# Two declarations moved in SBUF, so that matmul operands start at other offsets within a partition of SBUF

## What is computed

```python
xn = _layernorm(x)                       # x: (8, 512, 256)
# attention: q, k, v are two-layer nets with gelu
q = gelu(xn @ W1q + b1q) @ W2q + b2q     # k and v alike
scores = einsum('bid,bjd->bij', q, k) / sqrt(256 * 512) * tril(ones)
s = layernorm(einsum('bij,bjd->bid', scores, v)) * ln_w + ln_b
# feed-forward: weights quantised to -1, 0, 1 by their mean absolute value
h = relu(xn @ quant(W1).T + b1)          # 256 -> 1024
g = silu(h @ quant(W2).T + b2)           # 1024 -> 256
out = x + s * g
```

## The kernel before

| tensor | role in matmuls | before | after |
|---|---|---|---|
| `w_hi`, `w_lo`, `w1q` | stationary in L1, K, F1; moving in V (`w_*`) | 352 | 928 |
| `w2q` | moving in Y | 352 | 928 |
| `v_hi`, `v_lo` | moving in O | 352 | 416 |
| `x_all`, `xn`, `y`, `gw`, `v32` | none in the loop | 352 | 416 |
| `ident`, `ones`, `ones_r` | stationary in D (`ones_r`) | 128, 640, 128 | the same |
| `xT_*`, `g_*`, `r_*`, `z_*`, `e_*`, `s_*` | all the others | 928 | 928 |

## Time and profile before

### The profile page before, as it was taken

How to read it: one execution, slowest core, us unless ns; L and a number is a source line. 1 busy time by engine, 2 the same in 40 slices (tenths; PEclk the granted TensorE clock), 3 DMA queues, 4 the chain that set the end, 5 groups by cost and what they waited for, 6 DMA issues and landing times.

```text
span 312.9 us, 5715 instructions
## 1 busy us (share of the span) xinstructions
PE 306.3 (98%) x1874; PEld 272.8 (87%) x1874; DVE 248.0 (79%) x539; ACT 222.0 (71%) x420; POOL 133.3 (43%) x103
## 2 busy tenths in 40 slices
PE   8999999999999999999999999999999999999994
PEld 7688899888997899888997889978998889978894
DVE  3869988975899579895889759895798958596687
ACT  3486957959488667859489494886678595795862
POOL 2843673349060670509333390606705093313200
PEclk9799999999999999999999999999999999999999
DMA  7930035410004100050003200041000400020001
GB/s 249 372 121 0 2 111 157 136 70 0 2 2 138 63 0 0 34 168 0 0 0 125 76 0 0 0 138 63 0 0 35 167 0 0 0 69 2 0 2 67
DMA packets 15086, 18.54 MB, mean 59 GB/s; under 512 B 1761, under 2 KB 12513, under 8 KB 15074
## 3 DMA queue, kind: packets, MB, share of 16 engines
q1 hardware_dynamic: 14512, 17.98, 17.2%
q10 hardware_dynamic: 562, 0.41, 0.4%
HBM read 14.17 MB, written 4.22 MB: 59 GB/s over the span
## 4 chain that ended last, share of the span: by engine, by line
PE 74%; DVE 9%; issue 9%; POOL 4%; ACT 2%; DMA 1%; DVEq 0%; POOLq 0%
PE bank L810 73%; DVE gw L731 4%; POOL gw L359 2%; POOL o_rstd L353 2%; DVE g_lo L617 1%; DMA x_all<-in_x 1%; ACT o_square L484 1%; PE bank L792 1%; DVE e L642 1%; DVE x_all L733 1%; PE bank L839 1%; ACT o_var L487 1%; DVE gw L716 1%; DVE x_stats L547 0%; DVE gw L755 0%
## 5 line engine op out<-in xcount | busy, mean ns | idle before, releaser
L697 DVE TENSOR_TENSOR r_lo<-bank,r_hi 128x512 fp32r<-128x512 f32 x64 | 43.9, 691 | 34.4 <-ACT bank L464 34.4
L463 ACT ACTIVATE r_hi<-bank,col 128x512 fp32r<-128x512 f32 x64 | 47.0, 734 | 23.3 <-PE bank L810 23.3
L353 POOL TENSOR_TENSOR o_rstd<-o_var,neg_half 128x2 f32<-128x2 f32 x16 | 11.2, 699 | 82.2 <-ACT o_var L487 82.2
L464 ACT ACTIVATE bank<-bank,col 128x512 f32<-128x512 f32 x64 | 45.4, 709 | 0.0
L317 POOL TENSOR_TENSOR y<-y,xn 128x512 f32<-128x512 f32 x12 | 20.4, 1704 | 57.2 <-DMA xn<-x_norm_rows 57.2
L810 PE MATMUL bank<-xT_hi,w1q 128*128 128x512 f32 x128 | 39.8, 392 | 0.0
L810 PE MATMUL bank<-xT_lo,w1q 128*128 128x512 f32 x128 | 39.7, 392 | 0.0
L471 ACT CAST s_hi<-s 128x512 fp32r<-128x512 f32 (+3 forms) x32 | 14.8, 461 | 31.2 <-DVE s L685 28.5
L440 ACT ACTIVATE g_hi<-bank,col 128x512 fp32r<-128x512 f32 x48 | 33.8, 704 | 4.0 <-PE bank L810 3.6
L810 PE MATMUL bank<-w2q,r_lo 128*128 128x256 f32 x256 | 35.1, 280 | 0.0
L810 PE MATMUL bank<-w2q,r_hi 128*128 128x256 f32 x256 | 34.4, 277 | 0.0
(11 more groups left out here) (136 smaller groups left out, 707.8 us busy)
## 6 DMA issues: line engine op xcount, KB each, us to landing
out<-x_all SPq DMA_DIRECT2D x15, 256.0 KB, 2.2
x_all<-in_x SPq DMA_DIRECT2D x7, 512.0 KB, 3.5
y<-in_x_t SPq DMA_DIRECT2D x6, 512.0 KB, 3.8
xn<-x_norm_rows SPq DMA_DIRECT2D x6, 512.0 KB, 3.4
x_all<-in_w1t SPq DMA_DIRECT2D x2, 512.0 KB, 7.6
x_all<-in_w2t SPq DMA_DIRECT2D x1, 1024.0 KB, 10.3
x_all<-in_x SPq DMA_DIRECT2D x1, 256.0 KB, 3.3
x_all<-in_x ACTq DMA_DIRECT2D x1, 256.0 KB, 3.7
```

The costliest lines, as they stand in the source:

```text
L353: nc.gpsimd.tensor_tensor(o_rstd[:, half], o_var[:, half], neg_half[:, half], ALU.pow).then_inc(o_rstd_made, 1)
L463: nc.scalar.activation(r["hi"][:, f], pre[:], ACT.Relu, bias=b1)
L464: nc.scalar.activation(pre[:], pre[:], ACT.Relu, bias=b1).then_inc(f1_whole, 1)
L697: nc.vector.tensor_tensor(r["lo"][:, f], bank[(AT_F1 + f) % BANKS][:], r["hi"][:, f].bitcast(FP32), ALU.subtract).then_inc(r_split, 1)
```

## The change

Two declarations move. `causal` (512 bytes) goes from ahead of the weights to behind them, and `x_part` (64 bytes) from behind the large tensors to ahead of the weights. So the weights start 448 bytes lower, the tensors from `x_all` to `x_stats` start 64 bytes higher, and everything from `x_norm` on stays where it was. No instruction, wait, shape or order is changed on any engine.

```diff
         ones_r = sb("ones_r", [P, P], FP32R)
-        causal = sb("causal", [P, P])
         neg_half = sb("neg_half", [P, TT])
...
         d_const = sb("d_const", [P, 1])
+        x_part = sb("x_part", [P, 4, TT])
         w = {"hi": sb("w_hi", [P, 5, CK, C], FP32R), "lo": sb("w_lo", [P, 5, CK, C], FP32R)}
         w1q = sb("w1q", [P, CK, F], FP32R)
         w2q = sb("w2q", [P, FT, C], FP32R)
+        causal = sb("causal", [P, P])
...
         x_stats = sb("x_stats", [P, TT, 6])
-        x_part = sb("x_part", [P, 4, TT])
```

## The result

The changed kernel takes 318.38 us (median of 4 runs, 317.54 to 319.55) against 314.11: a ratio of 1.014, with a 95% interval of 1.010 to 1.018. Six later runs gave 1.012 (1.008 to 1.017). It is slower. My forecast was 313.1, and the case that came true is rival 2 in kind, with the 256-column products slower by more than it said and the 512-column ones faster.

The account below looks back on a forecast made before the run. PE's matmul pace was taken as the bound, except for 12.5 us per batch that DVE sets. Terms -0.8 + 0 - 0.1 + 0 = -0.9 us from the profiled 314.6 gave 313.7, as median 313.1 us; range 309.8 to 317.6.

Parts of the forecast that it names:

- rival 2: Equal offsets keep weight load and stream in each other's way, V, Y, O slow: 316.5 to 319.7 us, chance 0.21.
- What bounds the kernel: PE, busy 98% of the span: its matmul pace and its waits set the end, outside a DVE-set stretch per batch.
- the 12.5 us that DVE sets: Per batch, third tile of O to end of L1: PE has 0.37 us of slack or more, DVE sets K's start.
- term 3: L1, last Y, rest of O: gain 0.1 us in the first two batches; a 0.25 us loss per batch stays covered.
- Term 1: K and F1: 352 matmuls of 512 columns go from 229.0 to S's 226.7 ns, 0.8 us less.
- Term 2: V, Y and O in PE's own stretch, 648 matmuls of 256 columns: no change, 0; bounds 2.5 us more, 2.7 less.
- the other terms: K and F1 0.8 us less, L1 0.1 us less, moved tensors of the other engines 0.
- the bound of 118.0: V, Y, O: upper bound if about 540 matmuls went from 113.4 to 118.0 ns, 2.5 us more.
- one without a row: The forecast case: 512-column matmuls take S's pace, 256-column ones keep theirs, 313.1 us, chance 0.38.
- Rival 1: Offsets mean nothing to PE, both paces are a matter of phase: same time as before, 314.0 us, chance 0.22.
- Rival 3: Faster than S shows: 512-column matmuls go on towards 213 ns, the 118 spells vanish; half-way 309.4 us, chance 0.19.
- The signs I had named for rival 2: 8 matmuls of Y take 0.94 us instead of 0.91, and the weight loads' wait for `g_lo` shrinks.

## Why the prediction was wrong, point by point

**What bounds the kernel** held: the pace of PE outside the 12.5 us that DVE sets. The part of the loss behind that cover was hidden: it took 0.20 us a batch out of PE's wait (21 and 16 matmuls by 6.6 ns, less what L1 gained), where term 3 had worked out 0.25 for its own loss.

**Term 1**, K and F1 at S's pace, held in sign and nearly in size: 227.7 ns over F1's 30 (226.7 would have been 6.80 us, it was 6.83), and 226.7 in L1. But the row it rested on was partly luck. S stands at a distance of 0 in both kernels, and its six matmuls of 512 columns take 1.36 us (226.7 each) in batch 4 before and 1.38 or 1.39 (231) in batches 1 and 3 before and in every batch of the changed kernel. In the batch I read, S had the pace at which the long products settle.

**Term 2** is the step that failed: "I take no change: 0". The 256-column products went to 120.0 and stayed there. Over the 540 fast matmuls that I had counted this is 540 x 6.6 = 3.6 us. Less the 0.9 of the other terms, and with 37 x 6.6 = 0.2 us for the end of the first batch, where PE's wait gives no cover, it makes 2.9 of the 3.3 to 3.5 measured level by level. The starts in the trace of the later run of the changed kernel, whose clock is like that of the trace before (0.995 and 0.994) and whose span is 3.3 us longer, give the whole sum. From the first matmul of V in batch 0 to the last matmul, V takes 0.84 us more, Y 2.93, O 1.38 and S 0.19; F1 and K take 0.50 less, and L1 with the wait behind it 1.37 less: 3.5 us, of which 0.1 come back behind the last matmul. So the other terms gave less than 0.9: F1 and K 0.5, of which S took 0.2 back.

I had S in hand, the one product with a distance of 0, and it said 118.3. I put that down to the start of a run, because V also spends its first six matmuls near 118. (For Y this was misread: its first eight take 0.99 us, 124 ns each.) That was half right, and the reason why even the bound of 118.0 was too low: S's six and V's first six still take 0.71 us in the changed kernel, so 118.3 was indeed the start, but what follows at a distance of 0 is not 113.4, it is 120.0.

**The weighing of chances** was off with it. Nothing in the trace of before spoke for 113.4 at a distance of 0; every row with that pace had 192. I gave the case with the only row beside it, rival 2, a chance of 0.21, and 0.38 to one without a row.

**The rule of the Trainium skill** that I had weighed, "SBUF — State Buffer", section "Who interferes with whom" (PE's two reads have ports of their own, and PE never waits on anyone), would have given 0 and 314.0 us. The measurement decides against what I drew from it, that offsets can't change the time: the same instructions take 113.4 or 120.0 ns as the moving operand and the stationary one stand 192 or 0 bytes apart, and the fast pace comes back both with the weights at their old place and with the operands against them moved. Whether the two reads meet at all, no run shows.

**Rival 1**, that phase alone makes the pace, fell too, though spells by phase exist. **Rival 3** did not show in any of the distances tried: no product settled clearly below 227 ns for 512 columns or 113 for 256. The signs I had named for rival 2 came: 8 matmuls of Y in 0.96 us rather than 0.91 (0.94 was named), and the wait for `g_lo` shrank to 1.6 us. **The range** ended at 317.6 since I priced rival 2 at its middle and cut it there; its upper end, 319.7, would have held the time, though for a wrong reason, since it had K and F1 slower. One of its sums does not come out either: at 4.6 ns each, even all 648 matmuls would cost 3.0 us and the 540 that ran at 113.4 would cost 2.5, under the 3.1 that are 1%. So 118 as the pace could not by itself carry the change beyond 1%.

What stays open is the mechanism. That the place of two operands relative to each other decides is shown; that 448 acts as 192, 576 as 64 and 512 nearly as 0 speaks for a period of 256 bytes, and the 512-column products, 229 at 64 and 233 at 192, against one of 128. That the stream of one matmul and the weight load of the next reach for the same part of the memory at once is my reading of it, argued and not shown. Nor do the runs say why 256 columns want 192 or 64 and 512 columns 0 or 16, what picks between 113.3 and 117.8 in one layout, or whether it is the distance or the cut tile that loses all 16 bytes beside 192.

## What to carry to other kernels

Where PE is the bound and each matmul has its own weight load, the byte offsets of the two operands in a partition can matter: here they were worth 6% of the pace of the 256-column products (113.3 against 120.0 ns), 3% of that of the 512-column ones (226.7 against 233) and 1.1% of the kernel's time. Read that pace from starts, not from recorded durations, and look in the trace for the same shape at other distances before anything is moved; then try a few distances, for each width apart. Read every batch, since one layout can show two paces. Making all operands stand alike was, with 96 bytes apart, the worst choice for the 256-column matmuls here. When a row shows a pace only in short runs, take it as a case with a row behind it, and ask what a longer run would settle at, on both sides.

## What the hardware showed that I had not expected

- Of ten distances tried with 256 columns, two reached 113.3 ns, 192 and 64, and the others had 116.7 to 120; 512 columns settled at 226.7 at 0, at 226.7 or 228.4 at 16, 229 at 64, and 233 at 32, 96, 128, 192 and 224.
- For one layout PE has more than one steady pace. V of batch 1 in the kernel before ran at 118 throughout, V of batch 4 at 113.3 after its first six; at a distance of 64 the 48 of Y ran at 117.8 and the 16 behind O at 113.3. At distance 0 this choice is gone: every batch of the changed kernel has 120.0.
- Moving all large operands by 32 or 64 bytes together left V, Y and F1 of batch 4 as they were, to 0.01 us over 18 to 32 matmuls.
- The prologue's stretch at 1.2 GHz puts the runs of one program on levels about 1.5 us apart. Two profiled executions are compared only after it is taken out, best by the length of a batch in the middle.
